# Decay exponents of a decoder block: one half-array product per half of the heads in place of two full-array products

## What is computed

```
cum   = cumsum(ld, axis=1)                       # ld < 0, one number per position and head
dd    = cum_h[:, :, :, None] - cum_h[:, :, None, :]
Lmat  = where(tril, exp(dd), 0.0)
M     = einsum('blhn,bmhn->bhlm', c, b) * Lmat
Y     = M @ v_h
```

## Time and profile before

| | |
|---|---|
| median of three runs | 873.61 us |
| span of the profiled execution (first to last instruction) | 869.8 us; the page gives no other time for that execution |
| PE busy | 830.7 us, 96% |
| ACT busy | 736.7 us, 85% |
| DVE busy | 725.3 us, 83% |
| POOL busy | 166.0 us, 19% |
| mean granted TensorE clock | 0.983 |

### The profile page before, as it was taken

The page is one execution under the profiler, slowest core; times in us unless marked ns, Lnnn a source line. Parts: engine busy times, 40 slices in busy tenths (PEclk is TensorE's granted clock), DMA queues, the critical chain, the costliest instruction groups (busy, mean ns, idle before and its releaser), DMA issues.

```text
span 869.8 us, 21262 instructions
## 1 busy us (share of the span) xinstructions
PE 830.7 (96%) x7966; PEld 584.0 (67%) x7966; DVE 725.3 (83%) x2189; ACT 736.7 (85%) x1407; POOL 166.0 (19%) x198
## 2 busy tenths in 40 slices
PE   7899999999999999999999999999999999998874
PEld 4676767777767767777767767676767677654432
DVE  3653578989898999989898989999898988897775
ACT  3887789899898989899998989898998989784633
POOL 7101120312031131313120211312120310211110
PEclk9999999999999999999999999999999999998988
DMA  6100101010010101010100101001000000000000
GB/s 190 50 14 4 38 3 38 5 38 16 2 39 16 37 17 38 16 37 17 38 15 2 39 16 38 29 25 29 25 16 14 27 16 25 16 26 13 12 1 24
DMA packets 22403, 23.03 MB, mean 26 GB/s; under 512 B 11259, under 2 KB 13261, under 8 KB 22301
## 3 DMA queue, kind: packets, MB, share of 16 engines
q1 hardware_dynamic: 21868, 20.56, 7.8%
q10 hardware_dynamic: 432, 1.11, 0.4%
HBM read 16.68 MB, written 4.19 MB: 24 GB/s over the span
## 4 chain that ended last, share of the span: by engine, by line
PE 80%; ACT 7%; DVE 7%; issue 2%; DMA 1%; POOL 1%; SPq 1%; ACTq 0%; POOLq 0%; DVEq 0%
PE pM L2300 12%; PE pP L2252 8%; PE pP L2253 6%; PE pP L2254 6%; PE pDec L2287 3%; PE pY L2316 3%; PE pDec L2288 3%; PE pA L2379 3%; PE pA L2252 2%; PE pA L2351 2%; PE pC L2428 2%; PE pC L2388 2%; PE pA L2253 2%; PE pA L2254 2%; PE pD L2477 2%
## 5 line engine op out<-in xcount | busy, mean ns | idle before, releaser
L2252 PE MATMUL pP<-xn_hi,G_hi 128*128 128x256 f32 x512 | 163.0, 318 | 0.7 <-ACT P L737 0.7
L737 ACT ACTIVATE P<-pP 128x512 f32<-128x512 f32 x256 | 150.1, 599 | 7.8 <-PE pP L2254 6.6
L2253 PE MATMUL pP<-xn_lo,G_hi 128*128 128x256 f32 x512 | 143.8, 281 | 0.0
L2254 PE MATMUL pP<-xn_hi,G_lo 128*128 128x256 f32 x512 | 143.7, 281 | 0.0
L2300 PE MATMUL pM<-P,xnT 128*64 128x512 f32 x512 | 137.3, 614 | 1.9 <-DVE ML L1629 1.6
L599 POOL TENSOR_TENSOR rs_c<-ve_c,half_pow 128x4 f32<-128x4 f32 x48 | 49.1, 1023 | 405.0 <-DVE nm_c L1677 277.3
L2252 PEld LDWEIGHTS pP<-xn_hi,G_hi 128*128 128x128 f32 x512 | 96.5, 188 | 26.3 <-issue 13.9
L1629 DVE TENSOR_TENSOR ML<-pM,Lm 128x512 f32<-128x512 f32 x128 | 87.5, 684 | 22.1 <-PE pM L2300 19.2
L2253 PEld LDWEIGHTS pP<-xn_lo,G_hi 128*128 128x128 f32 x512 | 96.7, 189 | 2.9 <-issue 1.0
L2254 PEld LDWEIGHTS pP<-xn_hi,G_lo 128*128 128x128 f32 x512 | 96.5, 188 | 0.0
L746 ACT ACTIVATE Lm<-pDec 128x512 f32<-128x512 f32 x128 | 77.1, 602 | 21.3 <-PE pDec L2288 18.1
(11 more groups left out here) (242 smaller groups left out, 2026.1 us busy)
## 6 DMA issues: line engine op xcount, KB each, us to landing
x_in<-in_x SPq DMA_DIRECT2D x16, 256.0 KB, 3.3
cum_diag<-cum SPq DMA_DIRECT2D x256, 3.0 KB
x_res<-in_x SPq DMA_DIRECT2D x16, 256.0 KB, 2.6
ctxT<-in_ctx_t SPq DMA_DIRECT2D x16, 256.0 KB, 3.0
out_x<-r SPq DMA_DIRECT2D x16, 256.0 KB, 2.1
P<-in_wc ACTq DMA_DIRECT2D x2, 512.0 KB, 6.8
P<-in_wb SPq DMA_DIRECT2D x2, 512.0 KB, 8.6
fa<-in_w_t SPq DMA_DIRECT2D x1, 256.0 KB
```

The lines of the kernel that those rows point to most:

```text
L737: act.activation(P[:, half, 2 * pair:2 * pair + 2, 0:w], pP[k % 2][:, 0:2 * w].rearrange("p (h l) -> p h l", h=2), ACT.Copy).then_inc(p_co ...
L2252: pe.matmul(dst, w_hi, x_hi, start=True, stop=False)
L2253: pe.matmul(dst, w_hi, x_lo, start=False, stop=False)
L2254: return pe.matmul(dst, w_lo, x_hi, start=False, stop=True)
```

## The change

- The decay exponents come from one product per half of the heads: weights cum2 (64 output columns of that half), moving operand own_heads, a new buffer of 128 x 8192 bfloat16 that holds, for every sequence and half, the constant rows (-1 for the own head, identity and mask) and 24 rows that the DMAs fill with the head's sums. The two products of a unit write partitions 0-63 and 64-127 of pDec. PE's order of calls is not changed.
- cum2 gets rows of ones for the DMA's rows; ACT writes the sums into it directly (24 partitions by 1024 columns instead of 48 by 512). cum3, cum_diag, own_half and sel are gone, and so is POOL's spread_cum.
- c48 is laid out by halves; cum_transposed makes 8 transposes of 24 columns instead of 4 of 48.
- move_cum issues as many DMAs as before, each with 3 partitions of 8 pieces of 128 bytes instead of 6 of 4.
- Once, at the start, DVE fills own_heads with the constant rows (head_blocks), between cum_low(0) and head_low(3); the first move_cum waits for it. POOL's constants come in a new order, and six small loads are left out.
- qi is no buffer of its own but lies in the last two blocks of fa.

```diff
-CUM_ROWS = PARTS * H
+CUM_ROWS = PARTS * HH
-        c48 = sb("c48", [128, T, PARTS, H], BF16)
-        cum3 = sb("cum3", [CUM_ROWS, GS, L], BF16)
-        cum_diag = sb("cum_diag", [128, GS, HH, L], BF16)
+        c48 = sb("c48", [128, T, 2, PARTS, HH], BF16)
+        own_heads = sb("own_heads", [128, GS, 2, HH, L], BF16)
-        own_half = sb("own_half", [128, 128], BF16)
-        sel = sb("sel", [CUM_ROWS, HH + 2])
-        qi = sb("qi", [128, FB, GT], BF16)
+        qi = fa[:, 2:4, :, :].rearrange("p a b c -> p (a b c)").bitcast(BF16).rearrange("p (c w) -> p c w", c=FB)
...
                 if n == 0:
-                    sp.wait_ge(s_pool0, 12)
+                    sp.wait_ge(heads_ready, 1)
                 sp.wait_ge(dec_mm.sem, dec_mm.unit(FIRST_UNIT[n] + HALF * half - GS + HALF - 1))
                 mine = slice(HALF * half, HALF * half + HALF)
                 for hh in range(HH):
-                    sp.dma_start(cum_diag[hh:CUM_ROWS:HH, mine, hh, :], cum3[hh:CUM_ROWS:HH, mine, :])\
+                    sp.dma_start(own_heads[CUM_ROWS + hh:2 * CUM_ROWS:HH, mine, :, hh, :], cum2[n % 2][hh:CUM_ROWS:HH, mine, :, :])\
                       .then_inc(cum_moved[half].sem, 16)
...
-            def spread_cum(n):
-                pool.wait_ge(a_read.sem, a_read.at(n, A_CT))
-                pool.wait_ge(dec_mm.sem, dec_mm.at(n - 2, UNITS))
-                for h2 in range(2):
-                    last = pool.tensor_scalar(cum2[n % 2][0:CUM_ROWS, 0:seqs_in(n), h2, :], cum3[:, 0:seqs_in(n), :],
-                                              sel[:, HH + h2:HH + h2 + 1], None, ALU.mult)
-                last.then_inc(cum_spread.sem, 1)
...
             def place_cum(n):
                 act.wait_ge(a_mm.sem, a_mm.at(n, A_CT))
-                act.wait_ge(cum_spread.sem, cum_spread.at(n - 1, 1))
-                for moved in cum_moved:
-                    act.wait_ge(moved.sem, moved.at(n - 1, 16 * HH))
-                act.activation(flat(cum3[:, 0:seqs_in(n), :]), pA[0:CUM_ROWS, 0:width(n) // 2].bitcast(BF16), ACT.Copy)\
-                   .then_inc(a_read.sem, 1)
+                act.wait_ge(dec_mm.sem, dec_mm.at(n - 2, UNITS))
+                if n == 0:
+                    act.wait_ge(s_pool0, POOL_SETUP)
+                act.activation(cum2[n % 2][0:CUM_ROWS, :, :, :].rearrange("p s k l -> p (s k l)"),
+                               pA[0:CUM_ROWS, :].bitcast(BF16), ACT.Copy).then_inc(a_read.sem, 1)
...
+            def head_blocks():
+                dve.wait_ge(s_pool0, POOL_MASKS)
+                dve.tensor_copy(own_heads[:, :, :, :, :].rearrange("p s k h l -> p (s k) (h l)"),
+                                negR[:, :].unsqueeze(1).broadcast_to([128, 2 * GS, HH * L])).then_inc(heads_ready, 1)
...
                 if s == 0:
-                    pe.wait_ge(cum_spread.sem, cum_spread.at(g, 1))
+                    pe.wait_ge(a_read.sem, a_read.at(g, A_CT))
...
-                pe.matmul(pDec[:, :], own_half[:, :], flat(cum_diag[:, s, :, :]), start=True, stop=False)
-                pe.matmul(pDec[:, :], flat(cum2[g % 2][:, s, :, :]), negR[:, :], start=False, stop=True)\
-                    .then_inc(dec_mm.sem, per_unit(g))
+                for h2 in range(2):
+                    last = pe.matmul(pDec[64 * h2:64 * h2 + 64, :], cum2[g % 2][:, s, h2, :], flat(own_heads[:, s, h2, :, :]),
+                                     start=True, stop=True)
+                last.then_inc(dec_mm.sem, per_unit(g))
...
+                whole = pA[0:CUM_ROWS, :].bitcast(BF16).rearrange("p (s k l) -> p s k l", k=2, l=L)
                 for t in range(SIZES[n]):
-                    last = pe.transpose(pA[0:CUM_ROWS, 64 * t:64 * t + 64].bitcast(BF16), flat(c48[:, t, :, :]), id_b[:, :])
+                    for h2 in range(2):
+                        last = pe.transpose(whole[:, 2 * t:2 * t + 2, h2, :], flat(c48[:, t, h2, :, :]), id_b[:, :])
```

More of the change, by code:

```diff
@@ L321, in build @@
         const_ready = sem("constants_ready")
+        heads_ready = sem("head_blocks_ready")
         def sig(name, per):
@@ L343, in build @@
         p_copied = sig("p_copied", H)
-        cum_spread = sig("cum_spread", 1)
         cum_moved = [sig(f"cum_moved{i}", 16 * HH) for i in range(2)]
@@ L403, in build @@
         mask_rhs_s = x1[64:96, 0, 0:L]
-        dec_lhs_s, dec_rhs_s = x3[:, 1, :], o[:, :, :].rearrange("p a b -> p (a b)")
+        dec_rhs_s = o[:, :, :].rearrange("p a b -> p (a b)")
         ones, bv_cols, mem_exp_s, mem_mask_s = (u[:, 3, 128 * k:128 * k + 128] for k in range(4))
@@ L428, in build @@
         for part in range(PARTS):
-            here, there = slice(H * part, H * part + H), slice(32 * part, 32 * part + H)
+            here, there = slice(HH * part, HH * part + HH), slice(32 * part, 32 * part + HH)
             loads += [
-                (sel[here, :], dec_sel[there, :]), (dec_lhs_s[here, :], dec_lhs[there, :]),
                 (dec_rhs_s[here, :], dec_rhs[there, :]),
@@ L443, in build @@
         LOADED, LATER_LOADED = 16 * len(loads), 16 * len(later_loads)
-        POOL_TILES, POOL_SETUP, ACT_SETUP, DVE_MIDDLE, DVE_SETUP = 3, 18, 4, 4, 19
+        POOL_TILES, POOL_MASKS, POOL_SETUP, ACT_SETUP, DVE_MIDDLE, DVE_SETUP = 3, 9, 17, 4, 4, 19
         block = ctx.enter_context(nc.Block())
@@ L619, in _ @@
             rms_rsqrt(0)
-            pool.memset(own_half[:, :], 0.0).then_inc(s_pool0, 1)
             pool.memset(negR[:, :], 0.0).then_inc(s_pool0, 1)
@@ L623, in _ @@
                 pool.memset(cum2[i][:, :, :, :], 0.0).then_inc(s_pool0, 1)
-            pool.memset(cum_diag[:, :, :, :], 0.0).then_inc(s_pool0, 1)
+            pool.wait_ge(s_pool0, POOL_TILES + 3)
+            pool.wait_ge(s_w, LOADED)
+            pool.wait_ge(s_first, FIRST_LOADED)
+            parts = slice(0, CUM_ROWS)
+            pool.tensor_copy(negR[parts, :], dec_rhs_s[parts, :]).then_inc(s_pool0, 1)
+            pool.wait_ge(s_pool0, POOL_MASKS - 2)
+            pool.tensor_copy(negR[64:96, :].rearrange("p (h l) -> p h l", l=L),
+                             mask_rhs_s.unsqueeze(1).broadcast_to([32, HH, L])).then_inc(s_pool0, 1)
+            pool.wait_ge(s_pool0, POOL_MASKS - 1)
+            pool.tensor_copy(negR[MASK_ROWS, :], dec_rhs_s[MASK_ROWS, :]).then_inc(s_pool0, 1)
+            for i in range(2):
+                pool.memset(cum2[i][0:2 * CUM_ROWS, :, :, :], 1.0).then_inc(s_pool0, 1)
+            pool.wait_ge(s_pool0, POOL_MASKS + 2)
+            for i in range(2):
+                pool.tensor_copy(cum2[i][DIAG_ROWS, :, :, :].rearrange("p s k l -> p (s k) l"),
+                                 id_f[DIAG_ROWS, DIAG_ROWS].unsqueeze(1).broadcast_to([64, 2 * GS, L]))\
+                    .then_inc(s_pool0, 1)
+                pool.wait_ge(s_pool0, POOL_MASKS + 3 + i)
             for i in range(2):
@@ L628, in _ @@
             pool.memset(outT[:, :], 0.0).then_inc(s_pool0, 1)
[L629 to L644, removed]
             pool.wait_ge(s_pool0, POOL_SETUP)
             def fill():
-                spread_cum(0)
                 rms_rsqrt(1)
                 rms_rsqrt(2)
-                spread_cum(1)
                 stage_c_rsqrt(0, 1)
@@ L654, in fill @@
                 stage_c_rsqrt(0, 2)
-                spread_cum(2)
                 stage_c_rsqrt(0, 3)
                 stage_c_rsqrt(1, 1)
-                spread_cum(3)
                 stage_c_rsqrt(1, 2)
@@ L665, in body @@
                 last_rsqrt(g - 4)
-                spread_cum(g)
                 stage_c_rsqrt(g - 2, 2)
@@ L674, in drain @@
                 rms_rsqrt(13)
-                spread_cum(12)
                 stage_c_rsqrt(10, 2)
@@ L680, in drain @@
                 rms_rsqrt(14)
-                spread_cum(13)
                 stage_c_rsqrt(11, 2)
@@ L685, in drain @@
                 last_rsqrt(10)
-                spread_cum(14)
                 stage_c_rsqrt(12, 2)
@@ L691, in drain @@
                 stage_c_rsqrt(13, 1)
-                spread_cum(15)
                 stage_c_rsqrt(13, 2)
@@ L1602, in softplus_sum, with by_half @@
                    .then_inc(ld_ready.sem, 1)
+            def head_blocks():
+                dve.wait_ge(s_pool0, POOL_MASKS)
+                dve.tensor_copy(own_heads[:, :, :, :, :].rearrange("p s k h l -> p (s k) (h l)"),
+                                negR[:, :].unsqueeze(1).broadcast_to([128, 2 * GS, HH * L])).then_inc(heads_ready, 1)
+            def by_half(ap):
+                return ap.rearrange("p t (k h) -> p t k h", k=2)
             def cum_high(n):
                 dve.wait_ge(a_mm.sem, a_mm.at(n, A_CUM))
-                total = pA[:, 0:SIZES[n] * H].rearrange("p (t h) -> p t h", h=H)
-                high = c48[:, 0:SIZES[n], 0, :]
+                total = pA[:, 0:SIZES[n] * H].rearrange("p (t k h) -> p t k h", k=2, h=HH)
+                high = c48[:, 0:SIZES[n], :, 0, :]
                 dve.tensor_copy(high, total).then_inc(cum_hi_ready.sem, 1)
```

(9 more changed lines are left out.)

## The result

The changed kernel takes 875.34 us (median of 16 runs, 872.59 to 877.91) against 872.48 us of the kernel before on the same chip (16 runs): a ratio of 1.0030, 95% interval 1.0021 to 1.0039. The medians differ by 2.9 us, the ratio makes it 2.6. The kernel became slower, as forecast, and its time lies inside the range, but it lost only about half of the forecast 5.2 us.

A forecast was written before the change was run, and what follows sets the result against it. PE's own instruction stream was taken to bound the loop, with ACT 3 us below. Terms -0.6 + 5.2 + 0.4 - 1.0 + 0.65 + 0.5 = +5.2 us gave 875.0, plus 3.8 around the span 878.8 us; range 868 to 886.

The forecast's parts named there:

- The decays, -0.6 us: PE's 128 decay units: half-array pairs run side by side, but dearer changes of array shape leave only -0.6 us together.
- rival B: Decay products on PE: the pair doesn't overlap, each unit costs 0.21 us more, +27, 906 us; chance 0.05.
- A: Faster rival: the new decay weights' load hides behind a full-array product on PE, about 863 us; chance 0.13.
- the gain of 27 us: Decays on PE: two half-array products side by side stream 0.21 us less a unit, 27 us over 128 units.
- the forecast's classes: Decay units by PE neighbours: 53 at +0.112 us, 33 at +0.062, 23 at -0.237, 19 summing to -3.1 us.
- cum_transposed, +5.2: PE's transposes of the sums: four more and one more change of shape, 16 x 0.33 = +5.2 us.
- The third width: PE's transposes: 24 columns should run in a 32-wide shape, one more change at about 0.11 us behind scores.
- place_cum, +0.4: ACT's copy of the sums takes 0.99 us, +0.42 each; costed at +0.4 us in all, up to +3.
- POOL, -1.0: POOL's spreading goes; small POOL work queued behind it comes sooner, mattering in the drain: -1.0 us (0 to -3.1).
- later DMAs, +0.5: Moves of the sums land later against PE, tight in the drain: +0.5 us (0 to 2.5).
- Rival D: ACT or the start takes over: slower fill (+3.4 to 7.4) or late copy_p (+2.6), 882 to 888 us; chance 0.12.
- Start, +0.65: First DMAs wait for DVE's fill of own_heads (3.2 us, done at 33.6); first decay product 0.65 us later.

The follow-up runs named there:

- e5: Changed kernel with each decay unit as two full-array products again, zero blocks in cum2, as many DMA moves: 880.15 us, ratio 1.0084 to the kernel before.
- e1: Changed kernel with cum_transposed as 4 transposes of 64 columns again and place_cum as two ScalarE copies: 869.55 us, ratio 0.9969 to the kernel before.
- e8: Changed kernel with POOL's two spreading operations a group put back, into memory nothing reads: 875.79 us, ratio 1.0038 to the kernel before.

## Why the prediction was half right

**Bound.** Right: PE's order sets the loop, and the period grew by what its rows grew.

**The decays, -0.6 us: the step that failed, by its size.** The mechanism holds: the pair overlaps (rival B is out), a change of shape costs going in and coming out (A is out: a unit ends 0.337 after a full-array row, not 0.22), and the gain of 27 us goes into it. But the term measures -2.9 us (16 x 0.184, e5's period against the changed kernel's). Over all rows of the two profiled executions it is -2.7: the 128 units end 16.9 us sooner behind their predecessors, and the calls that follow them 14.2 us later. In a loop period the forecast's classes give 3 x 0.112 + 3 x 0.062 - 2 x 0.237 = +0.05 us; the rows give -0.19. Two rows of the kernel before that I had not looked at explain most of the difference, the row ahead of the unit in the earlier trace rows, and a unit with ffn_up behind it:

```profile
397.50 0.28 PE L2254 MATMUL pP<-xn_hi,G_lo 128*128 128x256 f32 x1
...
378.13 0.38 PE L2288 MATMUL pDec<-negR,cum 128*128 128x512 bf16 x1
378.29 0.50 PE L2477 MATMUL pD<-xq_hi,w 128*128 128x512 f32 x1
```
The same place in the changed kernel:

```profile
379.12 0.41 PE L2275 MATMUL pDec<-own_heads,cum 128*64 128x512 bf16 x2
379.45 0.50 PE L2467 MATMUL pD<-xq_hi,w 128*128 128x512 f32 x1
```
Four prices made it:

- The unit of before was put at 0.432 us, twice the 0.21 between its own two ends. From the row *ahead* of it, six of eight units (those behind head_pair and ffn_up) ended 0.448 (397.78 to 398.23 in the earlier trace rows): the first product already paid 0.232 there. I had not measured the first one's end, and "neither waits for weights" was wrong for it. 6 x 0.016 = 0.10 us a period.
- The way in: a unit of 0.343 taken, 0.337 measured; 64 columns load in 106 ns where I took 110. 8 x 0.006 = 0.05.
- The way out to ffn_up: 0.20 taken, 0.15 to 0.16 measured (the call grows from 0.511 to 0.666 us). Its first row ends 0.43 after the unit now, 0.20 above the 0.23 of such a row elsewhere, but it ended 0.28 after the unit of before: 0.05 was paid already. The calls of head_pair and project grow by 0.156 net, though the one behind a unit grows by 0.21; 0.05 comes back in a head_pair between head_values and attention scores, with no unit beside it (2.44 to 2.39), a share of luck. Together 0.09. To attend (0.198) and to transposes (0.15) it was right.
- Scores behind a decay, 0.15 less: right.

The sum, 0.24 us a period, is the miss in the loop; e5 confirms the term by undoing it. The first and the third are one oversight: prices of a change of shape were charged in full to neighbours that had paid a part of them before, at the change between float32 and bfloat16.

The Trainium skill ("TensorEngine Tiling (Array Packing)", Key Properties) says that a change of the tiling mode drains the TensorE; the trace agrees, with 0.12 us into 64 bfloat16 columns (0.337 less 0.216) and 0.15 to 0.20 back. Its Theoretical Speedup of up to 2x holds here for the streaming alone: 0.216 us a pair against 0.43.

**cum_transposed, +5.2.** Right: +0.330 us a group, 8 rows instead of 4 and one more change of shape; 5.3 us by e1. The third width was real: behind scores the eight rows take 0.11 us more than eight times 0.055, where the four of 48 columns took nothing more than their rows.

**place_cum, +0.4; POOL, -1.0; later DMAs, +0.5.** place_cum lasts 1.00 us as forecast (0.99), and the loop shows nothing of it: the periods of e5 and of the kernel before differ by 0.328, cum_transposed's 0.331. Rival D's late copy_p is out with it. POOL's gain isn't there in the loop, and too small to time in the drain (e8). One wait of decays for a DMA at the start, 1.7 us (1.6 before), and none behind it. The three were wrong singly and summed to -0.1, so by luck they cost the forecast nothing.

**Start, +0.65.** The fill took 2.29 us, not 3.2; the moves still began 0.77 later, behind place_cum, and the first decay at 41.91, 0.86 after the old 41.05 (0.65 forecast). One execution can't fix this term: in the profiled executions of all these kernels the first transposes of the sums end anywhere from 30.1 to 37.5 us. The +0.7 is therefore not shown. Rival D's start (a fill that ends behind 34 us) is out at 32.77. The Trainium skill ("VectorE: DVE Perf Modes", Side-by-side: where the cycles go) has four elements a cycle for such a copy, an estimate of 2.2 us; the trace agrees, with 2.29.

**The sum.** -2.9 + 5.3 + 0.7 = +3.1 us; timed +2.9, or 2.6 by the ratio. The two sure terms alone give +2.4, so the timing can't tell whether the start is in it. The profiled spans differ by 1.4, less than the timed medians; the changed kernel's profiled execution took 873.04 us, 2.3 below its median. That is also why the 3.8 us put around the span was too much: there it is 1.8.

## What to carry to other kernels

Price an instruction from the end of the row *ahead* of it to its own end, for each kind of neighbour, never from the distance within a group: 0.016 us at each of most units was a good part of this miss. Half-width products paid here where they stood next to others of the same shape (0.22 us a unit behind scores, 0.34 behind a full-array row), so count the borders between shapes, not the products. Before moving a call in a written order, check which buffer it fills and where the instruction that empties it stands in the *other* engine's order; and time each new order on the old kernel as well, since only the difference of the two tells what the change is worth.

## What was not expected of the hardware

- POOL's small power took 2.46 us beside DVE's fill of 128 x 8192; the other powers of this size take 1.0 to 1.43 us in the same trace. No run here shows why.
- One ScalarE copy of 24 x 1024 takes 1.00 us, two of 24 x 512 take 0.58 each.
- The issue of a DMA of 3 partitions took SP 0.75 us, for half the bytes as for the whole.
